# The unit-matrix matmuls into idle banks, and their waits, are taken out of the first stage of an attention and feed-forward layer

## Chip, cores and metric

The kernel runs on one core of a Trainium2 chip. The metric is the device time of one execution in microseconds, the median of three runs. TensorE is called PE here, VectorE DVE, ScalarE ACT, GpSimd POOL, and SyncE, which issues most of the DMAs, SP.

## What is computed

The input x has 2 sequences of 512 rows with 1024 channels; everything is fp32. The reference is a layer of two blocks with residuals:

```python
def _layernorm(x, axis=-1, eps=1e-05): ...
# block 1
x = x + _L0_xattn_ref(_layernorm(x, axis=-1), pos_BxS, ..., ctx_1024, ...)
#   qkv_in = rat_read(h, W, g, b, 3)      4 channels per head mixed, normalized
#   attention: 16 heads of 16, rope, causal mask, softmax over 512 keys
#   h = rat_write(h, attn_out, ...)       softplus, exp and a gated update
#   mlp_in = rat_read(h, ..., 2); mlp_out = silu(gate) * up   (weights: ctx_1024)
#   h = rat_write(h, mlp_out, ...)
# block 2
def _binary_diff_weight(w, base):
    d = w - base
    return base + jnp.mean(jnp.abs(d)) * jnp.sign(d)
gate = jnp.einsum('bsh,ih->bsi', hidden_states, W1)      # W1, W3: 3584 x 1024
up = jnp.einsum('bsh,ih->bsi', hidden_states, W3)
x = x + jnp.einsum('bsi,hi->bsh', jax.nn.silu(gate) * up, W2)
```

The three weights of block 2 are binary differences: their means of |w - base| need a pass over all of w1 and w3 before the first product with them.

## The kernel before

The program has two stages. The first one computes block 1 and, beside it, the means for block 2. The rows are cut in 8 tiles of 128. For each tile there are a `front` (layernorm, transposes, mixing by the diagonal matrices `diag`, normalization of the result `yn`, q, k and v by `wqkv`, rope, transposes), a `row` (the attention's output put back in rows), a `back` (rat_write of the attention, the second read), and a `finish` (rat_write after the small MLP, whose 32 pieces are called `mlp`). The attention runs over 16 groups of four heads and half a sequence. In it a `fill` of kind S writes scores by query into the four banks of `quad` (L1540, the causal mask is added by matmuls of `maskb` and `unit` at L1543), DVE takes their maxima (L2216, `negwide`), `turnmax` turns these (L1523), a `fill` of kind T writes the scores by key (L1550, L1555), ACT makes `prob` of them (L1864), and `weigh` multiplies with the values (L1513). `measure` is the load, difference and sum of |w - base| of one of 56 pieces of w1 and w3.

The order of all these on each engine is made before the program is built: `phase_one_order` places each part of each tile, taking at each step the part with the least start time less a hand-made lead, with a table of durations. It gives one list; each engine runs its own entries in that order, and waits on semaphores. `ffn_order` makes the list of the second stage, which computes block 2: 28 pairs of rows of w1 and w3 by a scheme with seven products (p1 to p7, L1606), then the product with w2 (L1653).

PSUM has 8 banks: `quad` holds banks 0 to 3, the two `pair` tensors banks 4 to 7. Each part that needs banks gets them from the order, and waits in `banks_free` for the reader of the last owner.

Into this order the kernel puts matmuls that compute nothing that is read. `unit` is the 128x128 identity in bf16. Before PE runs a part, `lull` looks for its key (stage, number, part) in the table `LULLS`. An entry (count, bank, user) means: wait until the bank is free for `user`, the part that gets the bank next, and then run `count` matmuls of unit with unit into it, of 512 columns. Where `user` is None there is no wait, the bank holds something else in its first half, and the matmul is of 256 columns, adding to its second half, which nobody reads. The table has 41 entries with 136 matmuls. 45 of them stand before parts of front 0 and front 1, at the start of the program.

```python
def lull(key):
    if key in LULLS:
        count, bank, user = LULLS[key]
        if user is None:
            unit_matmuls(count, bank, 2)
            return
        if user[0] == "fill":
            pe.wait_ge(at_m if SEQ_UNITS[user[1] - 1][0] == "S" else at_p, TURN[user[1] - 1] + 1)
        else:
            banks_free(pe, *user)
        unit_matmuls(count, bank)
```

In the profile these matmuls are L1449. The matmuls of `unit` with `maskb` in L1543 and L1555 are part of the computation and stay.

Of the kernel before, what the change touches and what calls it, by code (L numbers as in the profile page):

```python
# [674 lines left out]
def ffn_order():  # L675
# [190 lines left out]

LULLS = {
    ('front', 0, 4): (14, 0, ('front', 0, 11)),  # L870
    ('front', 0, 6): (14, 0, ('front', 0, 11)),
    ('front', 0, 11): (14, 0, ('front', 0, 11)),
    ('front', 1, 11): (3, 0, ('front', 1, 11)),
    ('turnmax', 3, 0): (4, 6, ('weigh', 5, 0)),
    ('row', 0, 0): (1, 6, ('row', 0, 0)),
    ('fill', 10, 0): (1, 4, ('back', 0, 0)),
    ('back', 0, 4): (1, 6, ('front', 5, 15)),
    ('fill', 14, 0): (1, 0, ('fill', 14, 0)),
    ('fill', 15, 0): (3, 6, ('weigh', 14, 0)),
    ('fill', 17, 0): (4, 4, ('front', 6, 13)),  # L880
    ('fill', 21, 0): (2, 4, ('turnmax', 7, 0)),
    ('turnmax', 7, 0): (2, 4, ('turnmax', 7, 0)),
    ('fill', 22, 0): (1, 0, ('fill', 22, 0)),
    ('weigh', 24, 0): (8, 4, None),
    ('weigh', 27, 0): (1, 6, ('turnmax', 10, 0)),
    ('turnmax', 11, 0): (1, 7, ('turnmax', 11, 0)),
    ('fill', 31, 0): (1, 0, ('fill', 31, 0)),
    ('fill', 32, 0): (1, 7, ('weigh', 31, 0)),
    ('row', 4, 0): (1, 6, ('row', 4, 0)),
    ('row', 4, 2): (4, 7, ('back', 1, 19)),  # L890
    ('back', 5, 4): (2, 4, ('weigh', 34, 0)),
    ('fill', 34, 0): (1, 4, ('weigh', 34, 0)),
    ('weigh', 34, 0): (9, 4, ('weigh', 34, 0)),
    ('fill', 36, 0): (4, 4, None),
    ('fill', 37, 0): (16, 4, None),
    ('fill', 38, 0): (1, 0, ('fill', 38, 0)),
    ('weigh', 38, 0): (6, 4, ('weigh', 38, 0)),
    ('fill', 41, 0): (2, 4, None),
    ('fill', 42, 0): (1, 0, ('fill', 42, 0)),
    ('finish', 0, 4): (1, 6, ('weigh', 42, 0)),  # L900
    ('fill', 46, 0): (1, 0, ('fill', 46, 0)),
    ('row', 6, 0): (1, 0, ('row', 7, 0)),
    ('back', 6, 0): (1, 0, ('row', 7, 0)),
    ('row', 7, 2): (2, 5, ('back', 7, 0)),
    ('back', 7, 4): (1, 6, ('mlp', 10, 0)),
    ('finish', 2, 4): (1, 3, ('finish', 3, 0)),
    ('finish', 4, 2): (1, 4, ('back', 7, 19)),
    ('finish', 4, 4): (1, 4, ('back', 7, 19)),
    ('finish', 5, 4): (1, 5, ('mlp', 25, 0)),
    ('turn', 0, 3): (1, 4, ('turn', 0, 3)),  # L910
}


def bass_layer(nc: bass.Bass, d: dict, out: bass.AP):
    with ExitStack() as whole:
# [521 lines left out]
        def _(pe):  # L1437
# [14 lines left out]
# [6 lines that stand above are left out]
# [1266 lines left out]
```

## Time and profile before

| what | value |
|---|---|
| median of 3 runs | 1232.62 us (1226.36 to 1236.79) |
| the profiled execution | 1234.41 us |
| its span, from first to last instruction | 1232.6 us |
| mean granted clock of PE | 0.989 |
| PE, DVE, ACT, POOL busy | 96%, 76%, 57%, 29% |
| DMA, mean over the span | 209 GB/s, 257.37 MB |

The span is the profiled execution without the 1.8 us around it. The first product of the second stage starts at 410.91 us. A granted clock of 1.00 is 2.4 GHz, 0.50 is 1.2 GHz; over the first 12 us the page shows 1.00 where no record of the clock stands. PE's busy time has the ends of its matmuls modelled: where two rows of PE overlap by 0.16 us, they run back to back.

### The profile page before, as it was taken

The page shows a single profiled execution, that of the slowest core. Times are in us where ns is not written, and L with a number is a line of the kernel's source. Part 1 is how long each engine was busy: PE and PEld are TensorE (multiplying, and loading weights), DVE is VectorE, ACT ScalarE, POOL GpSimd, SP SyncE. Part 2 cuts the span into 40 slices and gives each one's busy share as a digit, 9 for nine tenths or more (in the row PEclk, how much of TensorE's full clock was granted, in tenths as well). Part 3 has the DMA queues.
Part 4 walks back from the last instruction along what each step waited for, and adds up shares of the span by engine and source line. Part 5 has one row for each costly group of instructions (what it writes and reads, how often), then busy time and mean ns, then how long its engine had stood idle before and what let it go on. Part 6 is the DMA issues. An engine that isn't in the chain of part 4 may idle for free. (4 is left out here: it accounts for less than half of the span.)

```text
span 1232.6 us, 17284 instructions
## 1 busy us (share of the span) xinstructions
PE 1181.4 (96%) x6276; PEld 920.6 (75%) x6276; DVE 939.4 (76%) x1279; ACT 703.1 (57%) x1007; POOL 353.9 (29%) x441
## 2 busy tenths in 40 slices
PE   7988889999997999999999999999999999999998
PEld 4765554656775888878888888888788888888887
DVE  6778778778878867787777977778775777888864
ACT  4878667575557666557565666656655333334342
POOL 2233333423522334243553344433340000000000
PEclk8999899999999999999999999999999999999999
DMA  8366678865021257767687676776776968753232
GB/s 353 124 248 246 242 259 303 328 224 199 19 86 51 87 165 254 241 189 242 219 278 237 201 229 211 259 240 189 213 237 222 337 243 277 252 205 120 101 125 99
DMA packets 99065, 257.37 MB, mean 209 GB/s; under 512 B 9363, under 2 KB 23973, under 8 KB 98469
## 3 DMA queue, kind: packets, MB, share of 16 engines
q1 hardware_dynamic: 94948, 241.59, 54.6%
q0 software_dynamic: 4032, 14.68, 6.7%
q8 instruction: 50, 0.82, 0.3%
q14 instruction: 35, 0.28, 0.1%
HBM read 214.81 MB, written 41.42 MB: 208 GB/s over the span
## 5 line engine op out<-in xcount | busy, mean ns | idle before, releaser
L2585 POOL TENSOR_TENSOR raw_w<-raw_w,raw_base 128x256 f32<-128x256 f32 x224 | 197.2, 924 | 184.5 <-DMA raw_base<-in_mean_w 184.3
L2129 ACT ACTIVATE split<-grid 128x1024 fp32r<-128x1024 f32 x98 | 104.0, 1061 | 160.7 <-PE pair L1653 147.7
L2527 DVE TENSOR_TENSOR split<-grid,split 128x1024 fp32r<-128x1024 f32 x98 | 119.7, 1225 | 61.8 <-ACT split L2129 61.6
L1653 PE MATMUL quad<-split 128*128 128x512 f32 x588 | 149.3, 389 | 0.5 <-DVE hid L2534 0.5
L1653 PE MATMUL pair<-split 128*128 128x512 f32 x588 | 149.2, 389 | 0.0
L1653 PEld LDWEIGHTS quad<-split 128*128 128x128 f32 x588 | 110.4, 188 | 23.6 <-DVE split L2527 0.9
L1653 PEld LDWEIGHTS pair<-split 128*128 128x128 f32 x588 | 110.5, 188 | 22.8
L2308 DVE TENSOR_TENSOR ring_lo<-raw_base,ring_hi 128x1024 fp32r<-128x1024 f32 x56 | 70.0, 1251 | 33.1 <-ACT ring_hi L2074 27.1
L1606 PE MATMUL pair<-t_b_hi,ring_hi 128*128 128x512 f32 x224 | 89.0, 397 | 2.8 <-ACT snap L2093 2.7
L1606 PE MATMUL pair<-xnT_hi,ring_hi 128*128 128x512 f32 x224 | 87.4, 390 | 0.7 <-ACT t_b_lo L1981 0.7
L1606 PE MATMUL pair<-t_b_lo,ring_hi 128*128 128x512 f32 x224 | 87.8, 392 | 0.0
L1606 PE MATMUL pair<-xnT_lo,ring_hi 128*128 128x512 f32 x224 | 87.3, 390 | 0.0
L1606 PE MATMUL pair<-xnT_hi,ring_lo 128*128 128x512 f32 x224 | 87.2, 389 | 0.0
L1606 PE MATMUL pair<-t_b_hi,ring_lo 128*128 128x512 f32 x224 | 87.2, 389 | 0.0
L2304 DVE SCALAR_TENSOR_TENSOR raw_w<-quad,coeff,raw_base 128x1024 f32<-128x1024 f32 x52 | 66.5, 1280 | 19.6 <-ACT quad L1923 19.3
L2308 DVE TENSOR_TENSOR ring_lo<-raw_w,ring_hi 128x1024 fp32r<-128x1024 f32 x28 | 40.4, 1445 | 46.1 <-ACT ring_hi L1932 46.1
L1923 ACT ACTIVATE quad<-raw_w 128x1024 f32<-128x1024 f32 x52 | 53.1, 1022 | 26.7 <-POOL raw_w L2585 26.1
L2585 POOL TENSOR_TENSOR ctxw<-ctxw 128x256 f32<-128x256 f32 x56 | 44.1, 817 | 69.8 <-DMA ctxw<-in_mean_w 69.8
L2647 POOL DMA_DIRECT2D late<-in_w x28 | 24.9, 891 | 126.0 <-ACT late L2105 126.0
L2216 DVE TENSOR_REDUCE negwide<-quad 128x4 f32<-128x512 f32 (+3 forms) x32 | 46.9, 1488 | 13.2 <-PE quad L1543 13.1
L1606 PEld LDWEIGHTS pair<-t_b_hi,ring_hi 128*128 128x128 f32 x224 | 42.2, 188 | 13.4 <-ACT snap L2093 5.0
L1864 ACT ACTIVATE prob<-quad 128x1536 f32<-128x1536 f32 (+1 forms) x24 | 38.2, 1590 | 21.2 <-PE quad L1555 12.8
(338 smaller groups left out, 2759.6 us busy)
## 6 DMA issues: line engine op xcount, KB each, us to landing
raw_w<-in_w SPq DMA_DIRECT2D x56, 512.0 KB, 5.7
raw_base<-in_mean_w SPq DMA_DIRECT2D x56, 512.0 KB, 7.4
grid<-h_blocks SPq DMA_DIRECT2D x49, 512.0 KB, 3.7
ctxw<-in_w SPq DMA_DIRECT2D x28, 512.0 KB, 4.3
ctxw<-in_mean_w SPq DMA_DIRECT2D x28, 512.0 KB, 5.7
late<-in_mean_w SPq DMA_DIRECT2D x28, 512.0 KB, 7.5
late<-in_w POOLq DMA_DIRECT2D x28, 512.0 KB, 6.1
grid<-in_mean_w SPq DMA_DIRECT2D x28, 512.0 KB, 4.7
```

Of the source, the lines that this page charges most:

```text
L1606: a = pe.matmul(bank, ww[:, at + k, :], xx, start=first and k == 0 and n == 0, stop=k == half - 1 and n == 2, skip_group_check=not first)
L1653: a = pe.matmul(into[t], found[:, a, t * P:(t + 1) * P], found[:, b, :], start=p == 0 and n == 0 and q < 4, stop=p == PAIRS - 1 and n == 2 ...
L1864: act.activation(probs[TURN[u] % 2][:, :, 0:cols], quad[:, :, 0:cols], ACT.Exp).then_inc(at_p, 1)
L1923: act.activation(spare.rearrange("p a b -> p (a b)"), w[:, :], ACT.Sign).then_inc(f_sign, 1)
L2129: act.activation(splits[n % RINGS][:, 0:2, :], operands(n), ACT.Copy).then_inc(a_hi, 1)
L2216: a = dve.tensor_reduce(found.rearrange("p r j -> p (r j)"), quad[:, :, at:at + cols], AX.X, ALU.max, negate=True)
L2304: dve.scalar_tensor_tensor(w[:, :], sign, coeff[:, k:k + 1], base[:, :], ALU.mult, ALU.add).then_inc(f_w, 1)
L2308: dve.tensor_tensor(whole_of(pair[1]), source, whole_of(pair[0]).bitcast(F32), ALU.subtract).then_inc(done, 1)
L2527: dve.tensor_tensor(found[:, 2:4, :], operands(n), found[:, 0:2, :].bitcast(F32), ALU.subtract).then_inc(a_lo, 1)
L2585: a = pool.tensor_tensor(w[:, some], w[:, some], base[:, some], ALU.subtract)
L2647: pool.dma_start(lates[n % LATES][:, :], d["w2"][n], accum_op=ALU.add).then_inc(ld_add[n % LATES], 16)
```

## The change

The table is made empty. `lull` stays and finds no key, so PE runs neither the matmuls nor the waits in front of them. The table's 136 matmuls by key, cut:

```diff
-LULLS = {
-    ('front', 0, 4): (14, 0, ('front', 0, 11)),
-    ('front', 0, 6): (14, 0, ('front', 0, 11)),
-    ('front', 0, 11): (14, 0, ('front', 0, 11)),
-    ('front', 1, 11): (3, 0, ('front', 1, 11)),
-    ('turnmax', 3, 0): (4, 6, ('weigh', 5, 0)),
...
-    ('fill', 17, 0): (4, 4, ('front', 6, 13)),
...
-    ('weigh', 24, 0): (8, 4, None),
...
-    ('row', 4, 2): (4, 7, ('back', 1, 19)),
...
-    ('weigh', 34, 0): (9, 4, ('weigh', 34, 0)),
-    ('fill', 36, 0): (4, 4, None),
-    ('fill', 37, 0): (16, 4, None),
...
-    ('turn', 0, 3): (1, 4, ('turn', 0, 3)),
-}
+LULLS = {}
```

The file is 42 lines shorter above the program, so L1440 becomes L1398, and so on. PE's list has 2948 rows instead of 2989; the lists of DVE, ACT, POOL and SP have as many rows as before, 1123, 703, 146 and 484.

At the start of PE's list there stood (`hid` is the normalized tile, `xT` its transpose, `diag` the mixing matrices):

```order
L1449 MATMUL quad<-unit 128x512 x14
L1440 MATMUL pair<-ident,hid 128x128 x8
L1449 MATMUL quad<-unit 128x512 x14
L1478 MATMUL pair<-diag,xT 128x96 x8
L1440 MATMUL quad<-ident,hid 128x128 x8
L1449 MATMUL quad<-unit 128x512 x14
L1440 MATMUL quad<-ident,yn 128x128 x6
```

and now, on PE at the same place:

```order
L1398 MATMUL pair<-ident,hid 128x128 x8
L1436 MATMUL pair<-diag,xT 128x96 x8
L1398 MATMUL quad<-ident,hid 128x128 x8
L1398 MATMUL quad<-ident,yn 128x128 x6
L1436 MATMUL pair<-diag,xT 128x96 x8
```

The three groups of 14 are gone and the real rows follow each other as before. On PE around fills 36 and 37, in the second sequence's attention, there stood:

```order
L1690 MATMUL pair<-diag,xT 128x64 x8
L1449 MATMUL pair<-unit 128x256 x4
L1550 MATMUL quad<-big 128x256 x4
L1555 MATMUL quad<-unit,maskb 128x128 x4
L1550 MATMUL quad<-big 128x128 x4
L1555 MATMUL quad<-unit,maskb 128x128 x4
L1449 MATMUL pair<-unit 128x256 x16
L1540 MATMUL quad<-big 128x384 x4
```

and now:

```order
L1648 MATMUL pair<-diag,xT 128x64 x8
L1508 MATMUL quad<-big 128x256 x4
L1513 MATMUL quad<-unit,maskb 128x128 x4
L1508 MATMUL quad<-big 128x128 x4
L1513 MATMUL quad<-unit,maskb 128x128 x4
L1498 MATMUL quad<-big 128x384 x4
```

Here 4 and 16 unit matmuls are gone, and the fills stand next to each other.

## Rows read from the trace of the kernel before

**Rows 1.** The page's first part: busy time, share of the span, instructions.
```profile
PE 1181.4 (96%) x6276; PEld 920.6 (75%) x6276; DVE 939.4 (76%) x1279; ACT 703.1 (57%) x1007; POOL 353.9 (29%) x441
```

**Rows 2.** Stretches: from:to, length, busy time by engine, PE's clock, DMA share, GB/s.
```profile
26.00:50.00 24.00, 22.82 (x169) 19.89 (x171) 18.53 (x54) 21.55 (x42) 3.66 (x5) 1.00 0.21 80
50.00:80.00 30.00, 28.01 (x294) 20.82 (x286) 22.36 (x45) 24.34 (x48) 9.31 (x11) 1.00 0.78 282
80.00:200.00 120.00, 105.71 (x1011) 65.46 (x1009) 97.43 (x155) 83.83 (x148) 46.87 (x62) 0.96 0.70 251
200.00:235.00 35.00, 30.55 (x246) 18.24 (x247) 27.81 (x42) 22.99 (x41) 13.56 (x20) 1.00 0.92 328
300.00:411.00 111.00, 100.68 (x459) 75.36 (x458) 89.23 (x180) 67.02 (x116) 47.34 (x63) 0.95 0.22 83
411.00:1233.00 822.00, 814.97 (x3598) 671.65 (x3598) 617.31 (x669) 434.64 (x530) 208.10 (x236) 1.00 0.64 211
```

**Rows 3.** The same view of L1449 on PE alone, and its sum.
```profile
12.00:18.80 6.80, 4.13 (x10) 0.50 1.01 415
...
80.00:200.00 120.00, 10.44 (x37) 0.96 0.70 251
200.00:235.00 35.00, 7.45 (x39) 1.00 0.92 328
...
sum 411.00, PE 37.31; mean PE 4.15
```

**Rows 4.** Timeline at the start: start, us, engine, instructions, idle time before.
```profile
12.90 1.97 PE L1440 MATMUL pair<-ident,hid 128*128 128x128 f32 x8 [3.04 <-ACT hid L1824]
...
13.87 3.84 DVE L2370 TENSOR_TENSOR diag<-big,eye 32x768 f32<-32x768 f32 x4
...
14.66 5.25 PE L1449 MATMUL quad<-unit 128*128 128x512 bf16 x14
...
19.75 1.92 PE L1478 MATMUL pair<-diag,xT 128*128 128x96 f32 x16
...
21.51 1.04 PE L1440 MATMUL quad<-ident,hid 128*128 128x128 f32 x8
...
26.61 0.88 PE L1440 MATMUL quad<-ident,yn 128*128 128x128 f32 x6 [1.05 <-ACT yn L1837]
```

**Rows 5.** Short stretches of PE: length, busy time, clock, DMA share, GB/s.
```profile
131.50:134.90 3.40, 1.29 (x12) 1.00 0.53 177
134.90:141.70 6.80, 6.48 (x40) 0.50 0.63 233
182.70:186.10 3.40, 1.86 (x30) 1.00 0.50 188
186.10:189.50 3.40, 3.40 (x31) 0.50 1.01 386
...
209.90:213.30 3.40, 3.40 (x37) 1.00 0.89 299
219.70:223.10 3.40, 2.50 (x28) 1.00 0.88 267
```

**Rows 6.** The same view of L1449 alone in two of them.
```profile
209.90:213.30 3.40, 2.12 (x9) 1.00 0.89 299
219.70:223.10 3.40, 1.91 (x16) 1.00 0.88 267
```

**Rows 7.** Timeline of PE at three places with unit matmuls.
```profile
139.34 1.06 PE L1449 MATMUL pair<-unit 128*128 128x512 bf16 x2
...
222.56 0.93 PE L1540 MATMUL quad<-big 32*128 32x384 f32 x8 [0.90 <-ACT prob L1864]
...
400.57 0.39 PE L1449 MATMUL pair<-unit 128*128 128x512 bf16 x1 [1.42 <-DVE wr_s L2278]
```

**Rows 8.** Timeline of PE: one value product at either clock.
```profile
187.40 1.51 PE L1513 MATMUL pair<-prob,vaug 128*32 128x256 f32 x16
...
229.84 1.07 PE L1513 MATMUL pair<-prob,vaug 128*32 128x256 f32 x16 [0.58 <-ACT prob L1864]
```

More of the change, by code:

```diff
@@ L865, in ffn_order @@
     return order
-LULLS = {
-    ('front', 0, 4): (14, 0, ('front', 0, 11)),
-    ('front', 0, 6): (14, 0, ('front', 0, 11)),
-    ('front', 0, 11): (14, 0, ('front', 0, 11)),
-    ('front', 1, 11): (3, 0, ('front', 1, 11)),
-    ('turnmax', 3, 0): (4, 6, ('weigh', 5, 0)),
[L875 to L879, printed above, removed]
-    ('fill', 17, 0): (4, 4, ('front', 6, 13)),
-    ('fill', 21, 0): (2, 4, ('turnmax', 7, 0)),
-    ('turnmax', 7, 0): (2, 4, ('turnmax', 7, 0)),
-    ('fill', 22, 0): (1, 0, ('fill', 22, 0)),
-    ('weigh', 24, 0): (8, 4, None),
[L885 to L889, printed above, removed]
-    ('row', 4, 2): (4, 7, ('back', 1, 19)),
-    ('back', 5, 4): (2, 4, ('weigh', 34, 0)),
-    ('fill', 34, 0): (1, 4, ('weigh', 34, 0)),
-    ('weigh', 34, 0): (9, 4, ('weigh', 34, 0)),
-    ('fill', 36, 0): (4, 4, None),
-    ('fill', 37, 0): (16, 4, None),
[L896 to L909, printed above, removed]
-    ('turn', 0, 3): (1, 4, ('turn', 0, 3)),
-}
+LULLS = {}
 def bass_layer(nc: bass.Bass, d: dict, out: bass.AP):
```

## Prediction

> **What bounds the kernel now.** I read first the head of the profile's page [rows 1]: PE is busy for 96% of the 1232.6 us span. Then the stretches [rows 2]. After 411 us PE is busy for 814.97 of 822.00 us with no unit matmul among its work: there a moment lost on PE is a moment lost at the end, and one that the first stage hands over late is passed on whole. The first stage is another case. Between 80 and 200 us PE shows 105.71 of 120 us and between 200 and 235 us 30.55 of 35, and 10.44 and 7.45 us of these are unit matmuls [rows 3]. So PE has real work for 95.27 + 23.10 = 118.4 of 155 us there, 76%, near DVE's 97.43 + 27.81 = 125.2 us, 81%. No engine is full: what sets the pace is a chain in which PE, DVE and ACT hand the four banks of scores to and fro. The 136 unit matmuls of the table are 37.31 us of PE's busy time [rows 3], and nobody waits for their results. The granted clock is at half between 134.9 and 141.7 us and between 186.1 and 189.5 us [rows 5], and falls again between 300 and 411 us, where its mean is 0.95 [rows 2].
>
> **What the change removes, and what that gives.** PE's list loses 41 rows of unit matmuls and the waits in front of them. Nothing else moves, on PE or on the other queues, so the DMAs are issued behind the same waits.
> The first question is whether a unit matmul ever made real work late. It did not where PE was idle again after the last unit: after the third group of 14, the next transposes still waited 1.05 us for ACT's yn [rows 4]; after the 16 at 219.75 us, PE waited 0.90 us for ACT's prob [rows 7]. By this test (PE stands idle behind the unit) 36 of the 41 groups lie in idle time, the first before the transposes at 12.90 us and the last at 400.57 us among them. The other five: the 14 before the first diag product; 2 at 139.34 us, on the half clock and so 1.06 us long [rows 7]; and 1, 1 and 9 at 177.1, 190.1 and 210.5 us, whose last one runs into real work by 0.2 us or less. Taking these out gives 1.06 us at 139 us at most, some 0.2 us each at the three others, and I take **-1 us** (between -2 and 0, as the real work there may itself have been waiting).
> The group of 14 at 14.66 us is the largest. Its real successor, the diag product, needs diag, which DVE starts at 13.87 us and finishes 3.84 us later, at 17.71 us; it started at 19.75 us [rows 4]. Without the units it can start 2.0 us sooner, but on the half clock: the eight transposes took 1.97 us on it at 12.90 us and 1.04 us at 21.51 us on the full one [rows 4], a factor of 1.9. The product's 1.92 us become an estimated 3.5 us, 17.8 + 3.5 = 21.3 us against 21.67 us: 0.4 us are won there.
>
> **What the clock takes back at the start.** The clock was at half up to 18.8 us and rose there, after PE had run unit matmuls for 4.1 us without a break, and it stood at full through 26 to 80 us with only the 3 units of front 1 there [rows 2 to 4]. Without the 45 units of the start the first dense real work begins at about 26.2 us with the transposes of yn that stood at 26.61 us [rows 4]. I expect the clock to rise on this work, since it rose at 189.5 us after 3.4 us of score, mask, value products and transposes alone [rows 5, 8]; so about 3.5 to 6 us run at half, and lose half of that, 2 to 3 us, of which the 0.4 us go off. **+2 us** (0 to +5: nothing if the chain over DVE, POOL and ACT hides it; 5 if the clock needs twice as long, as between 134.9 and 141.7 us, where it stayed low for 6.8 us).
>
> **What the clock takes between 80 and 235 us.** The rows to compare are stretches of 3.4 us [rows 5, 6]. Before the two falls shown PE had been busy for 1.29 us (131.5 to 134.9) and 1.86 us (182.7 to 186.1). With the units the stretches at 209.9 and 219.7 us show 3.40 and 2.50 us and a full clock; without their units 3.40 - 2.12 = 1.28 and 2.50 - 1.91 = 0.59 us are left, no more than before the falls. The six units in front of the value products at 229.84 us are a third such place [rows 8], and the table has groups of four before turnmax 3, fill 17 and row 4's second turn, and of eight before weigh 24. An estimate from the units' 10.44 us of 80 to 200 us [rows 3]: where the two stretches above had 2 us of units each, that is room for five such places. I expect **eight more** falls than before (4 to 12).
> The price of one is read from the fall at 186.1 us: the 3.40 us that PE ran there at half [rows 5]. The same kind of value products took 1.51 us in it and 1.07 us at 229.84 us on the full clock [rows 8], and transposes 1.9 times as long [rows 4]. Over the mix, at a factor of 1.7, 3.4 us hold 2.0 us of work at full clock: 1.4 us lost by PE. Eight make 11.2 us. How much of that reaches the end is the choice that decides. Against all of it: real work fills 76% of PE's time here; in 200 to 235 us the DMA engines are busy for 0.92 of the time [rows 2] and ACT waits for data that POOL and the loads bring, which no PE clock delays. For it: the fills of the score banks and the products with prob are links of the chain, and each of them gets longer. I take half, **+5.6 us** (0 to 11.2, and to 17 if half of the falls last twice as long, as the first did).
> From 235 to 411 us the units stand in ones and twos among products with 256 and 376 columns that keep PE busy by themselves: 0.
>
> **The sum**, against the profiled execution's 1234.4 us: -1 + 2 + 5.6 = +6.6 us, 1241.0 us. The median of before is 1232.62 us, so I forecast 1239 us, +0.5%.
>
> **A rule of the skill.** The trace shows transposes and small real products from 26 to 80 us at full clock [rows 2]. The Trainium skill, page TensorE: Matmul & The Clock Gate, section Part 4: PE-mode transpose, says that the full clock does not engage for the transpose mode, since it does not count as PE work in the same way. Whether real work of this kind also raises a clock that is low is open from the rows; by this rule it might not in the front, and that makes the last rival below. The row at 186.1 us, where scores and values are mixed with transposes, speaks for a rise.
>
> **The rivals.**
> Slower for good: the half-clock stretches lie on the chain of the scores and pass on whole, some last 6.8 us as the first did [rows 5]. Start +4, falls +11.2, and half of them twice as long +5.6, minus 1: +20 us, 1253 us. It decides from where 0.8 us of the 1.4 arrive at the end: 3 + 12 x 0.8 is over 1%, 12.3 us. For it: 24% of slack on PE is an average, and the waits of the fills for ACT's prob show a chain with little play. Against it: the three runs of before lie 10 us apart although all have the units, so a fall more or less may be worth 1 us or 2, yet the falls of the profiled run left its 1234.4 us near the middle.
> Nothing is lost: the clock falls at few new places, and what it costs lies in idle time. Then the gains stand alone, -1 - 0.4, and the sum is 1231 us. For it: 26 to 80 us without units. Against it: the stretches at 209.9 and 219.7 us, which without units are as sparse as those before the falls.
> The units did hold PE up, which I have bounded by gaps: if the waits in front of them also kept PE from work that was ready, more than 12 us could be won. Their idle time ahead is at most 1.42 us, at 400.57 us [rows 7], and the work behind waited on, so I see no place for it: 1218 us.
> The front stays low: no rise until the wide products after 80 us. PE has 22.82 + 28.01 = 50.8 us of work from 26 to 80 us [rows 2], at 1.9 times that is +46 us, of which the 3.2 us that PE idles there go off: 1275 us.
>
> **How the numbers follow.** Forecast (1233 to 1245 us) 0.53; slower for good 0.27; nothing lost 0.14; held up by the units 0.03; the front stays low 0.03. A measurement of this kernel tells about 1% from no change. Range: from the nothing-lost case with its lower bound, 1232.6 - 4 = 1228 us, to the slower case's 1253 us plus the 4 us by which single runs depart from the median, 1257 us. Slower by over 1% (above 1244.9 us): the second case and a tenth of the first, and the last, 0.35. Faster by over 1% (under 1220.3 us): 0.04. Within: 0.61.
>
> **What would show it.** Right: the clock at half from the first transposes until 29 to 33 us; eight to ten falls between 80 and 235 us against two; PE busy less by about 37 us less what the half clock adds; the products of the second stage starting at 413 to 420 us against 410.9 us, and from there the two traces in step. Wrong: falls in the same number but a second stage later by the whole 16 us (the chain had no play); or a clock that stays full between 200 and 235 us (then sparse work is enough for it); or a front at half until after 40 us.

## The result and the profile after

The changed kernel takes 1237.17 us in the median of nine runs (1233.89 to 1240.65); the kernel before, run beside it nine times, takes 1231.74 us (1226.36 to 1236.79). The ratio is 1.005 with a 95% interval of 1.0026 to 1.0074: +5.4 us, slower by less than 1%. A second set of six runs of the same kernel, below, gave 1.0092 [1.0061, 1.0122]. The two intervals overlap only from 1.0061 to 1.0074. The truth is some +0.7%, and the two sets do not tell more.

The profiled execution is the lowest of the nine, 1233.89 us with a span of 1232.1 us, no longer than before's 1232.6 us. So one trace against the other shows how time moves, and the size has to come from the runs.

The page's first part and the clock's line of the second part, which answer to [rows 1]:

```profile
PE 1155.5 (94%) x6140; PEld 912.0 (74%) x6140; DVE 939.8 (76%) x1279; ACT 703.0 (57%) x1007; POOL 356.1 (29%) x441
...
PEclk9999998899999999999999999999999999999999
```

136 matmuls fewer, and PE busy 25.9 us less, where the units had been 37.31 us [rows 3]: the other 11.4 us are real work that ran longer. The other engines did what they did before. The stretches, to be laid beside [rows 2], with the same columns:

```profile
26.00:50.00 24.00, 22.18 (x144) 20.00 (x145) 16.93 (x50) 20.13 (x40) 3.67 (x5) 0.93 0.20 79
50.00:80.00 30.00, 27.58 (x285) 20.82 (x284) 24.04 (x49) 23.60 (x44) 10.02 (x11) 1.00 0.69 255
80.00:200.00 120.00, 99.24 (x991) 63.10 (x989) 95.86 (x152) 84.75 (x151) 44.09 (x59) 0.96 0.69 253
200.00:235.00 35.00, 23.87 (x186) 13.09 (x190) 28.01 (x40) 20.22 (x37) 14.84 (x18) 0.85 0.84 312
300.00:411.00 111.00, 99.03 (x459) 74.76 (x458) 89.44 (x182) 68.11 (x120) 45.80 (x62) 0.98 0.25 93
411.00:1233.00 822.00, 816.56 (x3618) 673.72 (x3615) 621.77 (x679) 436.96 (x532) 210.32 (x240) 1.00 0.64 212
```

The clock tells the places: 0.93 from 26 to 50 us where it was 1.00, and 0.85 from 200 to 235 us, again against 1.00. Between 80 and 200 us it is 0.96 as before, and from 300 to 411 us it is higher, 0.98 against 0.95.

**The start.** The timeline of PE (start, us, instructions, idle time before), to be laid beside [rows 4]:

```profile
13.09 1.94 PE L1398 MATMUL pair<-ident,hid 128*128 128x128 f32 x8 [13.09 <-ACT hid L1782]
17.95 3.70 PE L1436 MATMUL pair<-diag,xT 128*128 128x96 f32 x16 [2.92 <-DVE diag L2328]
21.45 1.91 PE L1398 MATMUL quad<-ident,hid 128*128 128x128 f32 x8
26.60 1.43 PE L1398 MATMUL quad<-ident,yn 128*128 128x128 f32 x6 [3.24 <-ACT yn L1795]
...
30.72 1.04 PE L1398 MATMUL quad<-ident,hid 128*128 128x128 f32 x8
```

The diag product comes 1.80 us earlier and takes 3.70 us in place of 1.92, so it ends at 21.65 us where it ended at 21.67. The eight transposes of hid take 1.91 us at 21.45 us, and 1.04 us at 30.72 us: half clock at the first, full clock at the second. Between them the record of the clock, which begins at 23.4 us, has one stretch at full, in which PE is all but idle, and one more at half:

```profile
23.40:26.80 3.40, 0.20 (x2) 1.00 1.01 402
26.80:30.20 3.40, 3.40 (x18) 0.50 1.02 407
```

The transposes of yn start at 26.60 us and so run on the half clock (1.43 us for 0.88), 0.01 us off their old time. PE is then late by some 1.6 us: DVE's instructions after 30 us start that much later than the same ones of before.

**From 80 to 240 us.** Each fall of the clock, with the stretch ahead of it (from:to, length, PE busy, clock, DMA share, GB/s):

```profile
81.40:84.80 3.40, 1.48 (x19) 1.00 0.92 369
84.80:88.20 3.40, 3.40 (x35) 0.50 0.03 11
136.00:139.40 3.40, 0.97 (x16) 1.00 0.72 264
139.40:142.80 3.40, 3.32 (x26) 0.50 0.87 317
183.80:187.20 3.40, 1.86 (x32) 1.00 0.50 164
187.20:190.60 3.40, 3.40 (x36) 0.50 0.72 246
197.40:200.90 3.50, 1.94 (x26) 0.99 0.80 282
200.90:204.30 3.40, 3.22 (x18) 0.51 0.92 342
211.10:214.50 3.40, 2.17 (x20) 1.00 0.63 220
214.50:221.30 6.80, 4.64 (x34) 0.50 0.78 289
231.60:235.00 3.40, 1.41 (x24) 1.00 0.64 263
235.00:238.40 3.40, 3.40 (x21) 0.50 0.52 187
```

Six falls against two, 23.8 us at half against 10.2 [rows 5]: 13.6 us more, four stretches of 3.4 us. The falls near 139 and 187 us are those of before. The new ones are at 85 us and at three places after 200 us, where units had stood: the four before turnmax 3 (80.4 us in before), the four before row 4's second turn (197.9 us), the nine before weigh 34 (210.5 us, the first stretch of [rows 6]), and the six before weigh 38, the last value product of [rows 8] (227.8 us). Where the 16 before fill 37 had stood, the second stretch of [rows 6], the clock does not fall: it comes back to full at 221.3 us, ahead of that place, and stays there. Ahead of each fall PE is busy for 0.97 to 2.17 us of 3.4.

**What arrives.** Where the same instruction of DVE starts in both traces gives how late the kernel is: 1.6 us after 30 us, 2.2 at 70, 3.6 after the fall at 84.8, 2.0 after 140 (before had its own fall there, twice as long), 1.5 at 195, 4.0 at 205, 5.0 at 220, 6.0 at 240. After 312 us, where before falls and the changed kernel does not, it is 5.2 us, and the first product of the second stage:

```profile
414.56 0.47 PE L1564 MATMUL pair<-xnT_hi,ring_hi 128*128 128x512 f32 x1 [0.74 <-ACT t_b_lo L1939]
```

is 3.65 us later than 410.91. From there the traces are not in step: 3.6 us at 500, about 1.5 us at most places from 600 to 860 (0.2 to 2.1), and -0.5 us at the end. PE's waits from there on (engine, line, releaser; us, times, longest), in before:

```profile
PE pair L1606 <- ACT snap L2093: 2.7, 3, 1.3
```

and in the changed kernel, where no wait for snap is listed:

```profile
PE pair L1564 <- ACT t_b_lo L1939: 0.7, 1, 0.7
PE quad L1611 <- DVE hid L2492: 0.5, 1, 0.5
```

The second stage, whose instructions the change does not touch, took 4.2 us less in this execution. The experiments show that this varies from one execution to the next.

### The profile page after: what moved, and what is told of

It is laid out like the page before. It is cut to its first block, busy times and chain, and to the rows that moved or that the text cites. A ratio compares the mean times of both kernels' runs of the same rounds, so it can differ in the third digit from the quotient of the medians.

```text
span 1232.1 us, 17009 instructions
## 1 busy us (share of the span) xinstructions
PE 1155.5 (94%) x6140; PEld 912.0 (74%) x6140; DVE 939.8 (76%) x1279; ACT 703.0 (57%) x1007; POOL 356.1 (29%) x441
## 4 chain that ended last, share of the span: by engine, by line
PE 68%; DVE 2%; ACT 1%; issue 0%; ACTq 0%; DVEq 0%
PE pair L1564 31%; PE quad L1564 12%; PE quad L1611 11%; PE pair L1611 11%; PE quad L1545 1%; PE pair L1545 0%; PE quad L1764 0%; PE quad L1708 0%; DVE inner L2362 0%; DVE hid L2234 0%; DVE wr_a L2221 0%; DVE wr_q L2227 0%; ACT sgate L1993 0%; DVE grid L2508 0%; PE quad L1705 0%
## 5 line engine op out<-in xcount | busy, mean ns | idle before, releaser
L2266 DVE TENSOR_TENSOR ring_lo<-raw_w,ring_hi 128x1024 fp32r<-128x1024 f32 x28 | 37.2, 1327 | 45.2 <-ACT ring_hi L1890 45.2
L1564 PEld LDWEIGHTS pair<-t_b_lo,ring_hi 128*128 128x128 f32 x224 | 42.0, 188 | 9.9
```

What stands on the lines that cost most here:

```text
L1564: a = pe.matmul(bank, ww[:, at + k, :], xx, start=first and k == 0 and n == 0, stop=k == half - 1 and n == 2, skip_group_check=not first)
L2266: dve.tensor_tensor(whole_of(pair[1]), source, whole_of(pair[0]).bitcast(F32), ALU.subtract).then_inc(done, 1)
```

## The experiments

Twelve experiments, each beside runs of the kernel before on the same chip. "Clock" is the mean granted clock over a kernel's runs, against before's.

**1 and 2. The two halves of the table by place.** start_only keeps the first four entries, 45 units; rest_only the other 37, 91 units.

```diff
 LULLS = {                          # start_only
     ('front', 0, 4): (14, 0, ('front', 0, 11)),
...
     ('front', 1, 11): (3, 0, ('front', 1, 11)),
-    ('turnmax', 3, 0): (4, 6, ('weigh', 5, 0)),
...
```
```diff
 LULLS = {                          # rest_only
-    ('front', 0, 4): (14, 0, ('front', 0, 11)),
-    ('front', 0, 6): (14, 0, ('front', 0, 11)),
-    ('front', 0, 11): (14, 0, ('front', 0, 11)),
-    ('front', 1, 11): (3, 0, ('front', 1, 11)),
     ('turnmax', 3, 0): (4, 6, ('weigh', 5, 0)),
...
```

> The first four entries of the table (45 unit matmuls before parts of front 0 and front 1) are kept, the other 37 are taken out. Theory A, the clock: a half-clock stretch of 3.4 us costs 1.0 to 1.7 us and passes on whole, wherever it falls. Against after, the start saves 1.6 us; the places from 80 us on stay as in after, with four or five falls between 80 and 240 us. So +3.5 to +4.5 us against before. Theory B, the start alone carries it: within 1 us of before. Theory C, the falls between 80 and 240 us are hidden and the second stage makes the difference: also within 1 us of before, with falls in the trace and no lag behind before at 240 us.

> The first four entries (45 unit matmuls) are taken out, the other 37 are kept. Theory A: +1 to +2 us against before: DVE and PE 1.6 us behind from 30 us on and no further falls than in before after 80 us. Theory B (the start alone): +4 to +6 us. Theory C: +1 to +2 us in the first stage, and less at the end.

start_only: 1.0042 [1.0019, 1.0066], clock 0.983 against 0.992. So the 91 units behind the start are worth 5.2 us (2.3 to 8.1). rest_only: 1.0027 [1.0001, 1.0053]: the start is worth 3.3 us (0.1 to 6.5). They add up to 1.0069. The traces show each half where it belongs: in start_only the stretch from 200 to 240 us, with two falls (6.8 and 3.4 us long),

```profile
200.00:240.00 40.00, 30.83 (x220) 0.87 0.85 308
```

and in rest_only, at half from 25.9 to 32.7 us, and at full from 200 to 240 us as before:

```profile
200.00:240.00 40.00, 35.81 (x273) 1.00 0.92 336
```

**3. The waits without the units.** The entries stay, each with a count of 0, so that PE waits as before and runs nothing.

```diff
-    ('front', 0, 4): (14, 0, ('front', 0, 11)),
+    ('front', 0, 4): (0, 0, ('front', 0, 11)),
...
```

> All 41 entries are kept, with a count of 0: PE waits as before where the table names a part, and runs no unit matmul. Theory A (clock): as after, +4 to +7 us against before, with the clock at half up to 29 to 33 us and four to six falls between 80 and 240 us. Rival: if the waits in front of the unit matmuls cost time that after has won back, this is slower than after by 1 us or more; if it is the waits that keep the engines in step, it is as before, within 1 us.

1.0069 [1.0044, 1.0093], between the change's two sets and as much as the two halves of experiments 1 and 2 together, which ran on the same chip. Five of the change's six falls are there (85.5, 140.1, 187.9, 215.2, 235.7 us); the one at 201 us is not, and the one at 187.9 us lasts 6.8 us. The waits neither cost nor gave anything that shows within some 3 us: the effect is the matmuls'.

**4. The kernel before, once more.** No edit; it measures the method.

> The kernel before, unchanged, as a control and for a second profile of it. Ratio 1.000 within 0.3%. In the first profile the second stage held 2.7 us of waits of PE for ACT snap, of which after had none; if these belong to the kernel before, they stand here again, at 500 to 600 us and at 876 us; if they come and go with the transfers, they don't, and the span is then 1228 to 1231 us.

0.9994 [0.9974, 1.0014], 1231.64 us. Its trace has falls at 134.4, 185.6, 393.8 and 400.6 us as before has, none at 312 us, and two of its own, at 168.5 and 209.5 us. And at its start the clock is up before the first real work, with the same 14 units ahead of it that had not kept it up in [rows 4]:

```profile
4.94 4.73 PE L1449 MATMUL quad<-unit 128*128 128x512 bf16 x14 [4.94 <-DVE maskb L2339]
13.00 1.09 PE L1440 MATMUL pair<-ident,hid 128*128 128x128 f32 x8 [3.33 <-ACT hid L1824]
...
17.95 2.00 PE L1478 MATMUL pair<-diag,xT 128*128 128x96 f32 x16 [0.83 <-DVE diag L2370]
```

In the first trace the clock did rise during these 14: their weight loads start 0.43 us apart up to 8.2 us and four of them lie within 0.75 us from 8.62 us on. It fell again at 12.0 us, behind PE's wait from 9.86 us on. (Records of the clock stand there from 8.6 us on, and not only from 12 us on.) The second trace is 1.7 us ahead of the first for that, from the diag product on. So a trace's falls are in part chance: one or two of them more or less between two traces say nothing, and the profiled execution on which the prediction rests had drawn the slower start.

**5. A delay at the second stage's door.** The table empty but for one entry: 20 units in front of the first product of the second stage.

```diff
-LULLS = {...}
+LULLS = {
+    ('early', 0, 0): (20, 4, ('early', 0, 0)),
+}
```

> The table holds one entry alone: 20 unit matmuls of 512 columns into bank 4 right before the first product of the second stage. They hold PE up by 20 x 0.22 = 4.3 us, less the 0.7 us that PE waited there for ACT: 3.6 us on top of after. Theory A (what the first stage hands over late is passed on whole): 9 us slower than before, ratio 1.007. Rival (the second stage has play, from loads that bound it at 500 to 600 and at 860 to 880 us): as after, 5 us slower than before or less, ratio 1.004 to 1.005.

1.0114 [1.0078, 1.0149]. The delay in its trace:

```profile
412.69 4.49 PE L1409 MATMUL pair<-unit 128*128 128x512 bf16 x20 [0.65 <-ACT t_b_lo L1941]
416.83 0.58 PE L1566 MATMUL pair<-xnT_hi,ring_hi 128*128 128x512 f32 x1
```

4.1 us later than the units' start, and against the change's two sets (1237.17 and 1241.58 us) its median of 1243.55 us is 6.4 and 2.0 us longer. So the delay reached the end by the first set; by the second alone it is not shown, as the intervals overlap. In a pair of traces it need not be seen. This trace is also a third one of the changed first stage: 20.4 us at half between 80 and 240 us, three stretches more than before, and a first stage that ends 1.8 us behind before's (412.69 against 410.91 us).

**6 and 7. One part of the middle.** mid_only keeps nine entries with 44 units, from row 4 to weigh 38 (200 to 230 us).

```diff
 LULLS = {                          # mid_only, mid_again
...
     ('row', 4, 0): (1, 6, ('row', 4, 0)),
     ('row', 4, 2): (4, 7, ('back', 1, 19)),
...
     ('weigh', 38, 0): (6, 4, ('weigh', 38, 0)),
...
```

> The table holds its nine entries from row 4 to weigh 38 alone, 44 unit matmuls between 196 and 230 us. Theory A (each fall costs 1.0 to 1.4 us and passes on): after had three falls there, of 3.4, 6.8 and 3.4 us, that held it back by 4.2 us more at 240 us than at 200 us. They go, and one may stay: 3 to 4 us faster than after, 1.5 to 3 us slower than before. Theory B (these stretches are bounded by loads and by POOL, so the clock costs nothing there): as after, 5 to 6 us slower than before.

> The nine entries from row 4 to weigh 38 alone once more (44 unit matmuls, 196 to 230 us). The first time its trace had no fall at 200 to 240 us and held its distance there, while its time was no better than after's. Theory A (a fall passes on whole): 2 to 4 us faster than the repeated after. Theory B (what is won there is lost again later, in the waits of the second stage): level with it within 1 us, although its mean clock is higher by 0.003.

1.0052 [1.0031, 1.0074], and the same kernel again 1.0065 [1.0041, 1.0088]. The units do their work on the clock. In mid_only's trace:

```profile
200.00:240.00 40.00, 36.24 (x294) 1.00 0.87 326
```

against 0.83 in the change:

```profile
200.00:240.00 40.00, 28.87 (x206) 0.83 0.82 304
```

And inside these 40 us the lag behind before falls, from 5.0 us at 200 us to 4.0 at 240 (from 7.75 to 6.65 in mid_again), where in the change it grows from 1.5 at 195 us to 6.0. So within the traces the full clock there is worth some 5 us. The total shows none of it for certain: it is as slow as the change's first set and faster than its second by 0.3 to 0.4%, where the intervals overlap. Their other falls differ: both kernels ran 80 to 200 us at 0.93 and 0.91, the change at 0.96.

**8. The other part of the middle.** half_only keeps the 15 entries from turnmax 3 to fill 32, 32 units (80 to 200 us).

```diff
 LULLS = {                          # half_only
...
     ('turnmax', 3, 0): (4, 6, ('weigh', 5, 0)),
...
     ('fill', 32, 0): (1, 7, ('weigh', 31, 0)),
...
```

> The fifteen entries from turnmax 3 to fill 32 alone, 32 unit matmuls between 80 and 195 us. Theory A: the falls at 85 and 140 us go or get shorter, 1 to 3 us faster than the repeated after, 3 to 4 us slower than before. Theory B: level with after within 1 us.

1.0049 [1.0026, 1.0072]. No fall at 85 us; the lag is 1.1 us at 200 us and 2.7 at 240, after two falls (6.8 and 3.4 us long). Again the cause and the local effect are as expected. The total is level with the change's first set and 6.2 us below its second (1241.58 us, taken beside it), where the intervals just overlap.

**9. The units of the start, longer.** In the kernel before, the first group of 14 becomes 22: the clock then rises before the first real work.

```diff
-    ('front', 0, 4): (14, 0, ('front', 0, 11)),
+    ('front', 0, 4): (22, 0, ('front', 0, 11)),
```

> Before, with 22 instead of 14 unit matmuls in the first group, so that PE is busy from 4.85 us to the first transposes at 12.9 us. In the profile of before the clock fell again at 12.0 us, and in the second profile of it it did not, and PE was 1.7 us earlier from 20 us on. Theory A: the early fall goes in nearly all runs, 0.5 to 1.5 us faster than before. Rival: where the clock rises late, 22 of them at 0.43 us reach 14.3 us and hold the transposes up: no change, or 1 us slower.

```profile
4.89 7.66 PE L1449 MATMUL quad<-unit 128*128 128x512 bf16 x22 [4.89 <-DVE maskb L2339]
12.94 1.09 PE L1440 MATMUL pair<-ident,hid 128*128 128x128 f32 x8 [0.39 <-ACT hid L1824]
13.87 3.19 PE L1449 MATMUL quad<-unit 128*128 128x512 bf16 x14
17.89 2.00 PE L1478 MATMUL pair<-diag,xT 128*128 128x96 f32 x16 [0.83 <-DVE diag L2370]
```

The transposes take 1.09 us in place of 1.97, the second group 3.19 in place of 5.25, and so the diag product starts when diag is there, 1.86 us earlier than in [rows 4] and at full clock: 1.8 us ahead from there on. 0.9984 [0.9969, 0.9998], -2.0 us (-3.8 to -0.2). The second trace of before had this start by chance; the two other traces with 14 units there, those of start_only and of experiment 10, ran the transposes at half (1.97 us). With 22 both traces are at full. So the longer group does in both traces what 14 leave open, and an interval this near to 1 doesn't tell its gain well.

**10. Units at three places that had none.** Into the kernel before, ahead of its falls at 312 and 394 us:

```diff
+    ('back', 6, 12): (5, 3, ('finish', 3, 0)),
+    ('finish', 6, 0): (6, 1, ('finish', 6, 0)),
+    ('norm', 2, 1): (13, 0, ('norm', 3, 1)),
```

> Before, with three more entries where PE waits and the clock fell in it: 5 unit matmuls before back 6's transposes (idle 1.4 us before 311.9 us), 6 before finish 6 (idle 1.6 us before 377.0 us) and 13 before norm 2 (idle 3.1 us before 393.7 us). Theory A: the falls at 312 and 394 us go in most runs, at 1.0 to 1.2 us each, 1.5 to 2 us faster than before. Rival: PE has play there and the added matmuls run into real work: no change, or up to 1 us slower.

1.0014 [0.9999, 1.0028], not told from no change. Behind the five units the clock is up: the eight transposes of hid take 1.06 us, and the lag goes down by 0.9 us.

```profile
310.94 1.24 PE L1452 MATMUL quad<-unit 128*128 128x512 bf16 x5
312.48 1.06 PE L1443 MATMUL quad<-ident,hid 128*128 128x128 f32 x8 [0.30 <-DVE inner L2407]
```

That the units did this is not shown: of the twelve traces without them three fall there (before, start_only, long_first) and nine do not, before's second one and the changed kernel's among them. The six before finish 6 left the lag at -0.3 us, as it was. The 13 did harm:

```profile
394.91 4.63 PE L1452 MATMUL quad<-unit 128*128 128x512 bf16 x13 [4.65 <-DVE wr_s L2281]
399.38 1.91 PE L1732 MATMUL quad<-ident,work 128*128 128x128 f32 x16
```

They wait 4.65 us for their bank, whose last reader is DVE's wr_s, and the clock falls at 394.9 us, as the wait ends. Then they run for 4.63 us, 3.4 us of it at half, in front of transposes that could have gone: the lag goes from -0.3 to +2.6 us. A filler that starts when the idle time ends covers nothing and delays.

**11. The change, once more.**

> The changed kernel again, as a control beside the next two and for a second profile of it. 1.0045 within 0.25% if the first measurement held. Its second profile should show the clock at half until about 30 us, at least five half-clock stretches between 80 and 240 us, and PE behind before by 3 to 5 us when the second stage starts.

1.0092 [1.0061, 1.0122], 1241.58 us, clock 0.980 against 0.992. In its trace the span is 1241.8 us, and two stretches stand out:

```profile
161.90:172.20 10.30, 10.30 (x65) 0.50 0.83 303
216.50:237.00 20.50, 16.73 (x113) 0.50 0.92 351
```

Between 80 and 240 us it has 41.1 us at half, 30.9 more than before. Its lag is 2.7 us at 120 us, 5.9 at 130, 8.7 at 175, 12.1 at 230 and 11.9 at 420 us, where its second stage starts at 422.84 us.

**12. The longer first group and two of the added ones, together.** The kernel before with the group of 22 and the groups of five and six of experiment 10, without the 13.

```diff
-    ('front', 0, 4): (14, 0, ('front', 0, 11)),
+    ('front', 0, 4): (22, 0, ('front', 0, 11)),
...
+    ('back', 6, 12): (5, 3, ('finish', 3, 0)),
+    ('finish', 6, 0): (6, 1, ('finish', 6, 0)),
```

> Before, with 22 unit matmuls in the first group, 5 before back 6's transposes and 6 before finish 6, and not the 13 before norm 2, which in the run before waited for DVE's wr_s and then held PE up for 4.6 us. If the gains add: 2.0 us from the start, 0.9 us from the fall at 312 us: 2 to 3 us faster than before, ratio 0.9975 to 0.9985. If the two groups only fill idle time: 2 us, as with the long first group alone.

0.9977 [0.9961, 0.9993], 1227.86 us (1224.80 to 1232.08, 12 runs): 2.8 us (0.9 to 4.8) faster than the kernel before, and faster than the changed one. With the group of 22 alone it had been 2.0 us (experiment 9), and the intervals don't tell the two apart: that the five and the six add anything is not shown. In its trace:

```profile
17.79 2.00 PE L1480 MATMUL pair<-diag,xT 128*128 128x96 f32 x16 [0.84 <-DVE diag L2372]
...
310.57 1.24 PE L1451 MATMUL quad<-unit 128*128 128x512 bf16 x5
312.12 1.06 PE L1442 MATMUL quad<-ident,hid 128*128 128x128 f32 x8 [0.31 <-DVE inner L2406]
```

**The runs taken together.** Over 35 single runs of before, time and mean clock go together: -0.87 us for each +0.001, with a correlation of -0.68. 0.001 of 1235 us is 2.47 us at half in place of full, so a microsecond at half costs 0.35 us. The other two sets of before, of 24 and 19 runs, give 0.33 and 0.37 us. That the two go together does not say which makes the other; that it is the units that set both is what experiments 1 to 3 say.

The traces give it by another way, less closely. For each, the microseconds at half between 80 and 240 us above before's 10.2, and what its lag behind before grows by from 70 to 240 us:

| kernel | more at half, us | lag grows by, us |
|---|---|---|
| after_again | 30.9 | 9.6 |
| start_only | 13.9 | 2.8 |
| the changed kernel | 13.6 | 3.9 |
| waits_only | 13.6 | 3.6 |
| mid_again | 10.2 | 2.9 |
| late_delay | 10.2 | 1.7 |
| half_only | 6.9 | -0.3 |
| mid_only | 6.8 | 1.6 |
| before_again | 3.5 | 1.3 |
| late_cover | 0 | 1.9 |
| long_first | 0 | -0.7 |
| combined | 0 | -0.2 |
| rest_only | -3.4 | -0.3 |

A straight line through these and before itself has a slope of 0.28 us for each us (correlation 0.93), whatever the edit was, and of 0.21 without after_again; single ones lie up to 2.1 us off it. So a stretch of 3.4 us at half costs 0.7 to 0.9 us by the traces and 1.2 us by the runs of before.

The table also sorts by what was kept. The five traces with none of the units between 80 and 240 us have 10.2 to 30.9 us more at half, the five that keep all of them -3.4 to 3.5 us, and the three that keep a part 6.8 to 10.2 us.

## Why the prediction was right

The change costs what the clock takes, +0.5% in the first set, and the forecast's mechanism is the one that the runs show: the units kept the clock up, in idle time, and without them the half clock makes the chain longer. That the figure was met so closely is luck in part, since the same kernel gave +0.92% in the second set, and in the first set the terms were off in opposite directions: fewer falls than forecast, and a dearer start and probably dearer falls. By its own steps:

- **Overruns, -1 us.** Seen in the trace only as the lag that goes from 3.6 to 2.0 us around 140 us, of which before's longer fall there is a part. Not measured by itself. The rival that the units or their waits held PE up is out: with waits and no units the kernel is as slow as without both (experiment 3), and without the 91 units it is slower, not faster (experiment 1).
- **The start, +2 us.** Right: the diag product at 17.95 us for 3.70 us (I had 17.8 and 3.5), half clock until 30.2 us with a stretch at full between (32.2 and 32.7 in two other traces), and a lag of 1.6 to 2.3 us in the traces without the start's units. The runs give 3.3 us (0.1 to 6.5), more, and the reason may be experiment 4: against a start like that of before's second trace the lag is 3.3 us and up. The front did not stay low. The Trainium skill, page TensorE: Matmul & The Clock Gate, section Part 4: PE-mode transpose, says that the full clock does not engage for the transpose mode. Here it rose at 30.2 us, while PE ran the small fp32 product with diag behind the transposes of yn, and the transposes at 30.72 us ran at full (1.04 us). So transposes do run at the full clock in this trace, other than the page says; whether transposes alone would raise it, no row read here tells.
- **Eight more falls.** Too many for the profiled execution: four stretches of 3.4 us more. The second trace has nine, and late_delay's, with the same first stage, three. By the mean clock over the runs, the first set had 0.0070 less than before, 17 us, five stretches, and the second 0.0124 less, 31 us, nine. The number depends on the execution, which the prediction's single figure didn't say; its bounds of 4 to 12 hold all but the three. Of the places that it named, turnmax 3, row 4's second turn, the stretch at 209.9 us and the value products at 229.84 us had a fall; fill 37's at 219.7 us, fill 17 and weigh 24 had none in this trace.
- **1.4 us of PE each, of which half passes on.** The term that was probably too small: the runs of before give 1.2 us for a stretch and not 0.7, start_only 0.8 (5.2 us for 21 us at half, by its mean clock), and the traces 0.7 to 0.9. The costs of the other kernels can't be divided so, because the mean clock has no record of their start. So some 1 us passes on, and 0.7 is at the edge of what was measured. The chain over the score banks has less play than I took, although PE has real work for 76% of the time only. I had set the 24% that are left against the price; an engine's mean idle time says nothing of the play of a chain that it is in. With it the rival "slower for good" had its condition fulfilled by the runs of before (over 0.8 us passed on), and missed its 20 us because there were fewer stretches at half than its twelve, at less than its 1.4 us each. The lag grew by 3.9 us in the profiled execution, and by 9.6 us in the other, where I had 5.6 for both.
- **235 to 411 us, nothing.** Right within what traces tell; falls come and go there in both kernels (before has three, the change one). That the ones and twos kept any away doesn't show.
- **The second stage hands the lateness on whole.** Borne out by the first set's median in experiment 5 and not decided by the second's; wrong for a pair of traces: from its first product to the first with w2, it took 550.9 and 549.8 us in two traces of before, 546.7 and 548.1 in two of the change, 551.4 and 550.0 in the two of the middle part. "In step" was not to be seen.
- **The sum.** +6.6 us against the profiled execution, +0.5% against the median; +0.50% and +0.92% were measured, +0.69% as the sum of experiments 1 and 2. By these two the start cost 3.3 us where I had 2, and the rest 5.2 us where I had 4.6 with the overruns in it; the 4.6 had eight falls at 0.7 us in it, and start_only has about six at 0.8. In the first set of the change fewer falls made up for what the start, and probably each fall, cost more.

**Open.** What makes the second stage vary by 6 us, from 546.7 to 553.3 us, with the same instructions: PE's waits for snap (4.7 us in the longest, none in the shortest) are a part of it, and I don't know what sets them. Why the part of the middle that kept the clock full from 200 to 240 us did not give its 5 us back in the total: chance falls elsewhere and the varying second stage are enough to hide it, but that was argued, not shown. Why the changed kernel's two sets lie 4.4 us apart. And what decides whether a fall lasts 3.4 us or 20.5 us.

## What to carry to other kernels

In a stage bound by a chain of small steps over several engines, idle PE time is not slack: price a lower clock at more than half of what it adds to PE's work there (here some 1 us of 1.4), and expect the number of falls to change from run to run, so size it by the mean clock over many runs and use the trace for the place. Matmuls that nobody reads can be worth their slots where they fill idle time ahead of real work and end before it is ready; one that must first wait for a bank can start when the idle time is over, and then it is a delay. The best borne out of them here raise the clock before the first real work, while the program waits for its first data anyway.

## What the runs showed of the hardware

- The clock stayed at half for 20.5 us while PE was busy for 16.73 of them, and for 10.3 us with PE busy for all of it by the profile, in a kernel whose other trace has no such stretch. Half clock under real work does not have to end after the first 3.4 us.
- The page of the profile shows the clock at full over the first 23.4 us of the changed kernel, and the durations say otherwise: 1.94 us at 13.09 us for transposes that take 1.04 at full. The clock's records begin at 23.4 us there. A clock is believed where a known operation has the length that goes with it.
- The same program had its falls at different places: of before's falls four came again in its second trace, the one at 312 us and the half clock of the start did not, and two were new. In three traces of the changed first stage the half clock between 80 and 240 us came to 23.8, 41.1 and 20.4 us.
